# In 22 FFN groups the fourth tile of the residual add goes over ScalarE and GpSimd; start and stage change of the program written in another order

## What is computed

```python
x = x + 0.5 * ffn(layernorm(x), w_up, w_down)
x = x + rnn(layernorm(x), Wf, Wi, Wh)
x = x + 0.5 * ffn(layernorm(x), w_up, w_down)

def ternary_linear(x, w):                 # used twice in ffn, gelu between
    alpha = mean(abs(w))
    w_t = sign(w) * (abs(w) > 0.5 * alpha)
    rms = sqrt(sum(x * x)) / sqrt(d)
    return (x / (rms + 1e-8)) @ w_t.T

def rnn(x):                               # minLSTM form, in log space in the reference
    f, i = sigmoid(x @ Wf.T), sigmoid(x @ Wi.T)
    h~ = g(x @ Wh.T);  h_t = f_t * h_(t-1) + i_t * h~_t;  h_0 = 0.5
```

## Time and profile before

| | |
|---|---|
| median of 3 runs | 257.25 us |
| lowest, highest | 255.78, 257.27 us |
| profiled execution: its own time | 256.79 us |
| profiled execution: span of the core's instructions | 255.1 us |
| mean granted TensorE clock | 0.993 of 2.4 GHz |
| first FFN, recurrent layer, second FFN | about 9 to 102, 102 to 161, 161 to 252 us |

### The profile page before, as it was taken

How to read it: one execution, slowest core, us unless ns; L and a number is a source line. 1 busy time by engine, 2 the same in 40 slices (tenths; PEclk the granted TensorE clock), 3 DMA queues, 4 the chain that set the end, 5 groups by cost and what they waited for, 6 DMA issues and landing times.

```text
span 255.1 us, 9745 instructions
## 1 busy us (share of the span) xinstructions
PE 239.6 (94%) x3779; PEld 170.5 (67%) x3779; DVE 231.8 (91%) x732; ACT 221.8 (87%) x529; POOL 205.6 (81%) x358
## 2 busy tenths in 40 slices
PE   6969999999999999999999999699999999999994
PEld 5726787776778777575555544366768787777774
DVE  4897899999999998999999999987999999978885
ACT  2697989999999999969989987998899999999871
POOL 5787998878888867879999999679988887887233
PEclk9988999999999999999999999999999999999999
DMA  6990000000000000000000000000111121112114
GB/s 195 297 278 5 4 4 3 3 3 4 3 6 3 0 4 4 3 0 1 3 1 0 0 4 0 3 3 3 44 44 44 46 85 44 44 45 75 53 44 126
DMA packets 18077, 9.73 MB, mean 38 GB/s; under 512 B 624, under 2 KB 17904, under 8 KB 18032
## 3 DMA queue, kind: packets, MB, share of 16 engines
q1 hardware_dynamic: 17760, 8.98, 12.8%
q10 hardware_dynamic: 272, 0.13, 0.2%
HBM read 4.92 MB, written 4.19 MB: 36 GB/s over the span
## 4 chain that ended last, share of the span: by engine, by line
PE 45%; DVE 29%; ACT 9%; POOL 8%; issue 6%; DMA 1%; DVEq 0%; POOLq 0%; ACTq 0%
PE Y L608 16%; PE U L554 8%; PE G L586 7%; PE U L555 7%; DVE hidden L864 6%; DVE st L882 5%; ACT h_hi L396 5%; DVE h_lo L809 5%; POOL root L249 3%; PE T L535 3%; DVE X L838 3%; DVE cand L854 3%; DVE mv L771 3%; POOL xn L279 3%; ACT U L390 2%
## 5 line engine op out<-in xcount | busy, mean ns | idle before, releaser
L809 DVE SCALAR_TENSOR_TENSOR h_lo<-h_hi,U 128x1024 f16<-128x1024 f16 x63 | 76.5, 1216 | 10.5 <-ACT h_hi L396 9.7
L249 POOL TENSOR_TENSOR root<-mv,half 128x12 f32<-128x12 f32 (+1 forms) x31 | 65.0, 2096 | 9.9 <-ACT square_junk L440 9.2
L390 ACT ACTIVATE U<-U 128x1024 f32<-128x1024 f32 x63 | 64.6, 1026 | 9.4 <-PE U L555 8.7
L396 ACT ACTIVATE h_hi<-U 128x1024 f16<-128x1024 f32 x63 | 64.7, 1027 | 1.0
L608 PE MATMUL Y<-down_w,h_hi 128*128 128x128 f16 x496 | 59.6, 220 | 1.4 <-DVE X L838 1.0
L608 PE MATMUL Y<-down_w_half,h_lo 128*128 128x128 f16 x496 | 59.2, 219 | 0.0
L279 POOL TENSOR_SCALAR xn<-X,neg_mean,scale 128x128 f32<-128x128 f32 x120 | 52.6, 452 | 4.0 <-DVE scale L777 3.8
L554 PE MATMUL U<-xt_hi,up_w 128*128 128x512 f16 x128 | 49.0, 383 | 5.4 <-DVE h_lo L809 5.2
L608 PEld LDWEIGHTS Y<-down_w,h_hi 128*128 128x128 f16 x496 | 47.6, 98 | 3.7 <-DVE X L838 2.2
L555 PE MATMUL U<-xt_lo,up_w 128*128 128x512 f16 x128 | 49.0, 383 | 0.0
L608 PEld LDWEIGHTS Y<-down_w_half,h_lo 128*128 128x128 f16 x496 | 48.6, 98 | 0.4
(11 more groups left out here) (115 smaller groups left out, 421.8 us busy)
## 6 DMA issues: line engine op xcount, KB each, us to landing
X<-in_L_attn_x SPq DMA_DIRECT2D x16, 256.0 KB, 5.3
out_x<-X SPq DMA_DIRECT2D x14, 256.0 KB, 2.4
out_x<-X SPq DMA_DIRECT2D x3, 128.0 KB, 2.0
up_raw<-in_L_ffn_w_up SPq DMA_DIRECT2D x1, 256.0 KB, 4.4
down_raw<-in_L_ffn_w_down SPq DMA_DIRECT2D x1, 256.0 KB, 4.6
out_x<-X ACTq DMA_DIRECT2D x1, 128.0 KB, 2.1
gate_raw<-in_L_attn_Wh SPq DMA_DIRECT2D x1, 64.0 KB, 3.5
gate_raw<-in_L_attn_Wi SPq DMA_DIRECT2D x1, 64.0 KB, 3.4
```

The costliest lines, as they stand in the source:

```text
L249: eng.tensor_tensor(root[l][:, g % 2, :, 0:w], mv[l][:, cols(g), 1:1 + w], half[:, :, 0:w], ALU.pow).then_inc(root_done[l], 1)
L390: eng.activation(U[part][:], U[part][:], ACT.Gelu, scale=1.0 / XN_SPLIT).then_inc(gelu_done, 1)
L396: eng.mul(h_hi[:, F % 2, 2 * part:2 * part + 2, :], U[part][:], H_SPLIT).then_inc(h_hi_done, 1)
L809: vec.scalar_tensor_tensor(out=h_lo[:, F % 2, 2 * part:2 * part + 2, :], in0=h_hi[:, F % 2, 2 * part:2 * part + 2, :], scalar=-1.0 / H_SPL ...
```

## The change

In the 22 groups whose factor rides with another (`shared`), VectorE adds only three tiles. ScalarE, at the end of step k, multiplies the fourth tile of Y of group k - 2 by its factor into one of two SBUF tiles (`scale_tile`, `scaled_tile`), and GpSimd adds that to X (`add_tile`), behind the norm of its step, for group k - 3. New waits: ScalarE's step for the reciprocal, for `down_done` and for the tile of two before (`tile_added`); VectorE's add and TensorE's down for `tile_scaled`; bn_stats of the recurrent layer and the store of the result for `tile_added`.

The start: the second weight sum takes the place of two products of ones, eight products of ones are put behind the first up, the weights' limit is made before xt_hi, the copy of the gate weights goes behind group 0, and bn_stats and moments of groups 3 to 6 move forward. The stage change into the second FFN: the last four recurrent groups are written out by hand on all engines. The normalised group 32 (the first of the second FFN) is still made by GpSimd and ScalarE together; group 33, which both made before, is now made by GpSimd alone.

```diff
+        shared = [F for F in range(2 * groups) if rides_with(F)]
...
         def by_both(n):
-            return groups + 2 <= n < 2 * groups + 2
+            return groups + 2 <= n <= 2 * groups
...
+            def add_tile(F):
+                pool.wait_ge(tile_scaled, shared.index(F) + 1)
+                c = of_ffn(F) * TILES + TILES - 1
+                eng.tensor_tensor(X[:, c, :], X[:, c, :], scaled_tile[:, shared.index(F) % 2, :], ALU.add).then_inc(tile_added, 1)
...
             for g in range(2, 4):
+                ln_moments(0, g + 1)
                 norm(g)
-                ln_moments(0, g + 1)
                 ln_roots(0, g + 1)
...
+            norm(2 * groups - 2)
+            inject_step(groups - 4)
+            norm(2 * groups - 1)
+            ln_roots(2, 0)
+            inject_step(groups - 3)
+            norm(2 * groups)
+            inject_step(groups - 2)
+            ln_roots(2, 1)
+            inject_step(groups - 1)
+            norm(2 * groups + 1)
+            ln_roots(2, 2)
+            for q in range(groups):
+                if 3 <= q < groups - 3:
+                    ln_roots(2, q + 3)
...
+                if q + 2 < groups:
+                    norm(2 * groups + q + 2)
+                if q < 3:
+                    ln_roots(2, q + 3)
+                if q >= 3 and groups + q - 3 in shared:
+                    add_tile(groups + q - 3)
...
+            def scale_tile(F):
+                y_ready(act, F)
+                act.wait_ge(down_done, F + 1)
+                if shared.index(F) >= 2:
+                    act.wait_ge(tile_added, shared.index(F) - 1)
+                eng.activation(scaled_tile[:, shared.index(F) % 2, :], down_tile(F, TILES - 1), ACT.Identity,
+                               scale=y_factor(F, TILES - 1)).then_inc(tile_scaled, 1)
...
                 if F not in (0, groups) and not diagonal_by_max(F - 1):
                     sum_squares(F - 1)
+                if F - 2 in shared and F not in (groups, groups + 1):
+                    scale_tile(F - 2)
...
+            turned(2 * groups - 1)
+            gate(groups - 2, 0)
+            gate(groups - 2, 1)
+            norm_tile(2 * groups, 2)
+            norm_tile(2 * groups, 3)
+            gate(groups - 2, 2)
+            gate(groups - 1, 0)
+            turned(2 * groups)
+            last_moments(3)
+            gate(groups - 1, 1)
+            gate(groups - 1, 2)
             act.preload_act_table(ACT.Gelu)
-            for k in range(groups):
+            gelu(groups, 0)
+            h_high(groups, 0)
+            turned(2 * groups + 1)
+            gelu(groups, 1)
+            h_high(groups, 1)
+            for k in range(1, groups):
...
                 if 2 <= F < LAST and 0 in rows:
                     pe.wait_ge(ffn_added, F - 1)
+                    if F - 2 in shared:
+                        pe.wait_ge(tile_scaled, shared.index(F - 2) + 1)
...
             up(0, 1)
+            keep_busy(Y[:, 0, 0, :], 8)
...
             up(groups, 0)
+            turn_back(groups - 3)
+            up(groups, 1)
             turn(2 * groups + 1)
-            up(groups, 1)
+            turn_back(groups - 2)
             turn_back(groups - 1)
...
-                for t in range(TILES):
+                if F in shared:
+                    dve.wait_ge(tile_scaled, shared.index(F) + 1)
+                for t in range(TILES - 1 if F in shared else TILES):
...
+            scan(groups - 2)
+            low_part(groups)
+            candidate(groups - 1)
+            scales(2, 1)
+            add_rnn(groups - 3)
+            scan(groups - 1)
+            h_low(groups, 0)
+            low_part(groups + 1)
+            scales(2, 2)
+            add_rnn(groups - 2)
+            h_low(groups, 1)
+            add_rnn(groups - 1)
+            later_stats(2 * groups)
```

More of the change, by code:

```diff
@@ L309, in _ @@
             for g in range(2, 4):
+                ln_moments(0, g + 1)
                 norm(g)
-                ln_moments(0, g + 1)
                 ln_roots(0, g + 1)
+            norm(4)
             ln_moments(0, 5)
-            norm(4)
             ln_roots(0, 5)
             ln_moments(0, 6)
-            for s in range(3, 3 * groups):
-                k, r, q = s, s - groups, s - 2 * groups
-                if 3 <= k < groups - 3:
+            for s in range(3, groups + 12):
+                k, r = s, s - groups
+                if k < groups - 3:
                     ln_roots(0, k + 3)
-                elif groups - 3 <= k < groups:
+                elif k < groups:
                     rms_step(k - 2)
-                if 2 <= q < groups - 3:
-                    ln_roots(2, q + 3)
-                elif groups - 3 <= q:
-                    rms_step(groups + q - 2)
-                if s + 2 < 3 * groups and r != 1:
+                if r != 1:
                     norm(s + 2)
@@ L336, in _ @@
                     rms_step(groups - 1)
-                if 0 <= s - 12 < groups:
+                if k < groups and k - 3 in shared:
+                    add_tile(k - 3)
+                if s >= 12:
                     rnn_scales(s - 12)
@@ L496, in _ @@
             rnn_moments(5)
-            for r in range(2, groups):
+            for r in range(2, groups - 2):
                 turned(groups + r + 1)
-                if by_both(groups + r + 2):
-                    norm_tile(groups + r + 2, 2)
+                norm_tile(groups + r + 2, 2)
                 gate(r, 0)
                 gate(r, 1)
-                if by_both(groups + r + 2):
-                    norm_tile(groups + r + 2, 3)
+                norm_tile(groups + r + 2, 3)
                 gate(r, 2)
@@ L699, in _ @@
             turn_back(0)
-            for r in range(2, groups):
+            for r in range(2, groups - 1):
                 turn(groups + r + 1)
@@ L703, in _ @@
                     gate(r, n)
-                turn_back(r - 1)
+                if r < groups - 2:
+                    turn_back(r - 1)
+            gate(groups - 1, 0)
+            turn(2 * groups)
+            gate(groups - 1, 1)
+            gate(groups - 1, 2)
             up(groups, 0)
+            turn_back(groups - 3)
+            up(groups, 1)
             turn(2 * groups + 1)
-            up(groups, 1)
+            turn_back(groups - 2)
             turn_back(groups - 1)
@@ L958, in _ @@
             add_rnn(1)
-            for s in range(groups + 3, 2 * groups):
+            for s in range(groups + 3, 2 * groups - 2):
                 r = s - groups
-                if r == groups - 1:
-                    low_part(groups)
                 scan(r - 1)
@@ L984, in _ @@
                         scales(2, q + 3)
-                    if diagonal_by_max(F - 1) and F > groups:
+                    if diagonal_by_max(F - 1):
                         sum_squares(F - 1)
```

68 lines of the change are left out of this document (38 added, 30 removed).

## The result

The changed kernel takes 258.08 us (median of 20, 256.76 to 259.92) against 256.73 us (median of 20) for the kernel before on the same chip. The ratio is 1.0056, with a 95% interval of 1.0038 to 1.0073: 0.6% slower, less than the 1% that the forecast called the bound, but 2.4 us above the forecast of 255.7 and just outside the range of 253.6 to 258.0. The profiled execution took 258.28 us (span 256.5) against 256.79 (span 255.1).

What follows compares the result with a forecast made beforehand. The prediction took a two-group loop over ScalarE, VectorE and TensorE (5.39 us per group) as the bound, with VectorE bounding part of the first FFN. Gains of 0.4 + 0.9 + 0.2 = 1.5 us gave 255.7 us, range 253.6 to 258.0.

Steps and rivals of the forecast that it cites:

- The start: First FFN up to group 4's first gelu: 0.4 us gained, the rest lost to ScalarE waiting for late reciprocals.
- Groups 4 to 15: First FFN after the start: VectorE-bound steps go away, 0.9 us gained.
- then the loop from there: First FFN after groups 12 and 13: steps at the two-group loop's 5.39 us, group 15 1.3 us earlier than before.
- The way into the second FFN: From the last recurrent groups to group 20: the new order followed at old durations, 0.2 us gained.
- The stall ahead of group 19: Second FFN: group 16's scaled tile waits for group 5's den, making group 19's gelu 0.8 us late.
- Full gain: Rival: reciprocals come in time at both FFN starts, giving 253.6 us; chance 0.18.
- Groups 20 to 31: Rest of the second FFN: the loop's 5.39 us per group stands, nothing gained or lost.
- ScalarE did not become the beat: Rival: ScalarE sets group spacing, through a 0.38 us scaled tile or three waits, 5.46 us; 257.1 us, chance 0.16.
- GpSimd, level with it, did not either: Rival: GpSimd's round with the add sets group spacing, 5.75 us with a 0.72 us add; 260.5 us, chance 0.08.

Runs made afterwards that it cites:

- e3: Changed kernel with the old order on all engines from the last four recurrent groups to group 16's second gelu; 257.37 us, ratio to before 1.0031.
- e4: Changed kernel plus 13 unused fp32 products of ones filling TensorE's two gaps on the way into the second FFN; 256.63 us, ratio to before 1.0018.
- e2: Kernel before with only the sharing of the add, old start and old way into the second FFN; 257.56 us, ratio to before 1.0044.
- e5: Changed kernel with the sharing kept only in groups 0, 1 and 16, gaps not filled; 257.61 us, ratio to before 1.0072.
- e13: Changed kernel with filled gaps and no sharing in groups 0, 1, 9, 10 and 16; 255.14 us, ratio to before 0.9936.
- e6: Changed kernel with filled gaps and the sharing in all riding groups but 0, 1 and 16; 255.40 us, ratio to before 0.9953.
- e9: Changed kernel with filled gaps, tiles of groups 0, 1 and 16 scaled behind the next gelu instead of ahead; 255.30 us, ratio to before 0.9946.
- e14: Second run of e6 (filled gaps, no sharing in groups 0, 1 and 16); 254.90 us, ratio to before 0.9932.
- e7: Changed kernel without any sharing and with the 13 filling products; 255.62 us, ratio to before 0.9967.
- e8: Kernel before with the new start alone; 255.91 us, ratio to before 0.9978.
- e1: Changed kernel without the sharing, new start and new way into the second FFN kept, gaps not filled; 255.66 us, ratio to before 0.9986.

## Why the prediction was wrong

The forecast was -1.5 us; by its span the profiled execution gave +1.4, and the median +1.35. By the prediction's own parts:

**The start** was to bring group 4 0.43 us forward; it came 0.14 late. The mechanism was right: both stalls are in the places named, and the scaled tiles start at 29.33 and 35.40. The sizes were off by some tenths: the first scaled tile was to start at 28.8, with den ready at 28.5, and den was ready at 29.05. Of that, 0.27 us is that this execution's group 0 began later, with the clock at 0.50 from 9 to 12 us. In e3 and e4, which have the start of the change, groups 3 and 4 came at 29.15 to 29.18 and 35.23 to 35.26, near the 29.1 and 35.1 of the forecast. What the prediction did not see is that the sharing also forfeits good executions. It took group 2 at 24.34 as the start of before. In e2, which has the start of before and kept its clock, group 2 came at 22.84, and group 4 at 35.62 all the same; with the steps of before (5.30 and 5.89) it would have been 34.03, an estimate. The kernel before spans 253.6 us in its best executions, at full clock; the change, e2, e3, e4 and e5 never span less than 254.4.

**Groups 4 to 15** were to give 0.9; they gave 0.21. This is the first step that failed. The steps of 5.39 into groups 5 to 11 came true (37.76 us for seven, against 38.06 before). What failed is "then the loop from there": into groups 12 to 15 I expected 5.56, 5.56, 5.39 and 5.39, and it was 5.74, 5.53, 5.33 and 5.92, 0.6 more. The forecast has two faults there. First, groups 11 to 15 are not shared, so VectorE's steps with their four adds do not get shorter: the steps into groups 14 and 15 sum to 11.22 before, 11.25 in the change and 11.23 in e13, where I wrote 2 x 5.39 = 10.78. That is 0.47 of the 0.6. Second, I had taken the VectorE-bound steps as single steps to be shortened by 0.26, and ScalarE's delay of h_hi takes that back: e13 shows that sharing in groups 9 and 10 costs 0.27 rather than gains. Without those two, groups 4 to 15 give 0.48 (60.01 against 60.49).

**The way into the second FFN** was to give 0.2; it cost 1.44. This is the step that failed most. The term that was missing is the clock, put at nothing without a reason: I carried TensorE's durations over at full clock into a stretch in which the change makes two gaps, although shows the same engine at 0.50 behind a gap of 2.54 us. With the gaps filled (e4) the way in costs 0.12 instead of 1.44, and with the gaps open and the clock kept (e5, where only group 16 is shared) it gains 0.09. So 0.1 to 0.3 is error in the hand count of the order, and 1.3 to 1.5 is the clock. The stall ahead of group 19 was forecast at 0.8 and is 0.66. In the old order it costs nothing by group 20 (11.63 us from group 18 to 20 in e2, 11.64 before), as forecast; in the new order it does, 0.54 us (11.86 in e4, 11.32 in e6).

**The rivals.** "Full gain" (reciprocals in time at both starts) is what e9 makes by moving the three tiles. It was priced at 253.6 us and gives 255.3. In e9's profile group 4 came 0.45 us earlier than before, not 1.7, in an execution with the clock at 0.50 from 9 to 16 us; groups 4 to 15 gave nothing instead of 0.9, namely the 0.2 of the change less the tile of group 1, which is paid there; and the way in, filled, gave 0.7 instead of 1.1.

**Groups 20 to 31**: nothing, as forecast, at 5.39. ScalarE at 0.25 to 0.27 and GpSimd at 0.46 have the prices taken. So ScalarE did not become the beat, and GpSimd, level with it, did not either.

The terms add up: 0.6 (start) + 0.7 (groups 4 to 15) + 1.6 (way in) = 2.9 = 1.4 + 1.5. Shown by runs is that three scaled tiles ahead of three gelus carry the loss of the sharing (e5, e6, e9), that the clock on the way in carries about 1 us of the median (e4; e5 for the mechanism), and that both removed make the kernel 0.5 to 0.7% faster than before (e6, e9, e14), most of it by the new start and the filled way in (e7 has 0.3% without any sharing). No error hides another: all three have the same sign. Open is why an execution keeps or loses its clock, at the start and on the way in; e2, e3, e5 and e8 show that one order can do either. The start was not varied alone beyond e8, and three of e4's twelve executions, with a mean clock of 0.985 and spans of 255.7 to 255.9, are not explained by any trace.

## What to carry to other kernels

An instruction moved to another engine brings its waits into that engine's queue: look for the one place where its operand is late, ahead of what it stands, and put it one place later (e9 gained 0.7% over e4 by order alone). Ask of such an operand both what makes it late in the profiled execution and what would make it late in a better one: a second chain just under the first (here GpSimd's den, within 0.1 us) swallows every gain ahead of it. When a new order opens gaps on TensorE, price the work behind them at both clock levels, and fill them where the level decides; a profile that kept its clock does not show that the next execution will. Before a step is shortened on paper, check that the instructions that make it long are among those moved.

## What the runs showed of the hardware

- The same kernel loses TensorE's clock in some executions and not in others: ten of twenty for the change (mean spans 257.0 and 255.5), four of twelve for e1 (255.9 and 253.5). On the way in, the profiles of the change, e1, e3 and e8 show 0.50 for 3 us or more, those of before, e2 and e5 never, and none of the eight with the fill.
- With the same two gaps on TensorE, 1.33 and 1.73 us, e5 kept the granted clock at 1.00, and the change (1.34 and 1.73) fell to 0.50 behind them.
- Thirteen fp32 products of ones, 128x128 (five in 1.28 us, eight in 1.95; each shows as two matmuls), stood in those two gaps in eight profiles, all of which kept the granted clock at 1.00 there. They cost no time: the step from group 16 to 17 is 6.56 us with them in e4 and 6.58 without them in e5.
- An `ACTIVATE` of 128x128 from PSUM with a scale column is 0.36 to 0.40 long in its row, and the next instruction starts 0.25 to 0.27 us after it.
- A two-input fp32 add of 128x128 on GpSimd takes 0.46 us in the change; VectorE's multiply and add of such a tile takes 0.28 (24.2 us for 88, before).
